# Attention and quantized feed-forward block on one core: batch 1's rotary products on GpSimd, statistics in pairs, maxima 8 slots ahead

## Chip, cores and metric

The kernel runs on one core of a Trainium2 chip. The metric is the device time of one execution in microseconds (us); lower is better. Engines are named as in the profile: PE (TensorE), DVE (VectorE), ACT (ScalarE), POOL (GpSimd) and SP (SyncE, which issues the DMAs).

## What is computed

The input is `x` of 8 batches x 512 rows x 256 columns. The rows are normalised (layer norm without weights); the result feeds causal attention with 16 heads of width 16 and rotary positions, and a linear layer whose input and weight are rounded to fp8 with one scale per tensor. Both are added to `x`:

```python
xn = _layernorm(x, axis=-1)
x = x + _L0_attn_ref(xn, L0_attn_W_q, L0_attn_W_k, L0_attn_W_v, L0_attn_W_o) + _L0_ffn_ref(xn, L0_ffn_weight, L0_ffn_bias)
```

and inside the two:

```python
Qr = _rope(Qh, cos, sin)
Kr = _rope(Kh, cos, sin)
scores = jnp.einsum('bhqd,bhkd->bhqk', Qr, Kr) * DH ** (-0.5)
...
pattern = jax.nn.softmax(scores, axis=-1)
heads = jnp.einsum('bhqk,bhkd->bhqd', pattern, Vh)
...
xq = fake_quant_fp8(x)
wq = fake_quant_fp8(weight)
return jnp.einsum('bsd,od->bso', xq, wq) + bias
```

The scale of the fp8 rounding needs the largest absolute value over all eight batches.

## The kernel before

All engines have their own instruction list, written out in Python, and wait on each other by semaphores; an engine never passes an instruction that waits. After a prologue the lists run over **slots**. A batch n has 20 slots, 20n to 20n+19, five for each of its four groups of heads. In a slot PE computes scores of batch n transposed (`scores`, line 864, into the two banks `st_ps`), ACT takes the exponents of them (`exp`, line 724), POOL masks the diagonal (`mask`, line 465), and PE multiplies with the values three and six slots after a group's first slot (`first_block`, `other_blocks`, line 958).

The softmax needs the row maxima first. PE computes the scores once more the other way round, two banks per slot (`scores_for_max`, line 884, into the three banks `s_ps`), and DVE takes the maxima (`row_max`, line 607). This runs `LEAD` = 10 slots ahead of the exponents, so the slot loop begins at slot -10. When a group's maxima are complete, PE turns them (`turn_max`, line 936, item `"mt"`), DVE splits them in two bf16 parts (`split_max`, lines 640 and 642), and SP writes them as two extra rows under the queries (`shift_rows`, line 358); the first scores of that group wait for these DMAs.

The queries and keys of a batch come from a chain: PE projects (item `"qk"`, `project`, line 849), DVE multiplies with cosine and sine (`rope`, lines 555 and 556), then `rotate` (lines 307, 308), `high` (705), `remainder` (315), `middle` (710) and `low` (320) split the result in three bf16 parts, with w = 0 for queries and w = 1 for keys. From batch 1 on, POOL does rotate, remainder and low, and ACT high and middle. SP writes the parts to DRAM (`write_parts`, line 333) and reads them back in the layout of the scores (`read_stack`, line 349). Batch 0 has its own short chain ahead of the slot loop (`project_whole`, line 839).

Where the smaller pieces stand is a table, `OFFSETS` (line 48): an item and the slot, relative to 20n, at which PE does it. Items (`"qk"`, `"v"` values, `"o"` heads turned back, `"at"`, `"fin"` output, `"mt"`, `"spread"`) take two shared banks `m_ps` in turn, and `bank_free` (line 974) makes PE wait until the item two places earlier has been read by its reader: ACT for `"v"` (`copy_v`, line 731) and `"at"`, DVE for the others. `copy_v` stands in ACT's list one slot after its item. `copy_heads` (738) of the last group stands two slots into the next batch.

The prologue also has the row statistics of all eight batches (`statistics`, lines 533 to 541, DVE; `invert`, 434 and 436, POOL; `normalise`, 692, ACT; `turn_rows`, 829, PE; `copy_turned`, 699, ACT), spread over slots -10 to -3 for batches 3 to 7 (`TURN_SLOT`). The rounding of the normalised input runs over steps qv (ACT), qe, qc (DVE), qw, xq (POOL) at slots set by `quant_at` (line 105). In an engine's list a slot's pieces stand in a fixed order; on ACT it is: exponents of the slot, turned copies, qv, `copy_heads` of the last group, `copy_v` of the item one slot earlier, `copy_at`, the other `copy_heads`, and last high and middle of the chain.

## Time and profile before

| what | value |
|---|---|
| median of 3 runs | 444.62 us (443.45 to 444.95) |
| the profiled execution: its own time | 446.0 us |
| the profiled execution: span from first to last instruction | 444.0 us |
| busy share PE, DVE, ACT, POOL | 89%, 81%, 63%, 64% |
| mean granted TensorE clock | 0.965 |
| share of the chain that ended last: PE, DVE, ACT, DMA | 59%, 17%, 8%, 5% |

Busy shares are averages over stages that differ. The span has three: the prologue up to the first row maxima, a stretch in which maxima run without exponents and the first two batches settle, and then batches that repeat to a hundredth of a microsecond.

### The profile page before, as it was taken

To read this page: it belongs to the slowest core of one execution; us is meant where nothing else is said; L and a number is where in the kernel's file an instruction comes from. 1 tells how busy PE (TensorE), PEld (TensorE's weight loads), DVE (VectorE), ACT (ScalarE), POOL (GpSimd) and SP (SyncE) were. 2 spreads that over 40 slices of the span, in tenths; PEclk is the share of its full clock that TensorE was granted. 3 is DMA by queue.
4 is the path that set the end of the run, shared out by engine and by line. 5 is a ranking of instruction groups with operands and counts; after the bars stand their busy time and mean duration, and the time that the engine had idled before them with its cause. 6 is when DMAs were issued, how large, how long until landed. Compare 5 with 4: busy or idle time off the path is not lost.

```text
span 444.0 us, 9396 instructions
## 1 busy us (share of the span) xinstructions
PE 397.3 (89%) x2911; PEld 234.7 (53%) x2911; DVE 359.3 (81%) x1372; ACT 278.9 (63%) x505; POOL 282.8 (64%) x284
## 2 busy tenths in 40 slices
PE   7905778987989999999999999999999999999886
PEld 7504553443645655565656565565555554555435
DVE  1997789999797879988898889888988898779314
ACT  3564758564773777567765766677747766657651
POOL 2575685367576678668767786687866764236670
PEclk9956899997998999999999999999999999999999
DMA  8939425833186047733675257623970497020111
GB/s 265 290 130 230 68 74 135 162 62 120 53 162 145 2 131 203 141 54 120 178 140 90 73 172 157 128 74 118 192 144 21 149 211 144 9 95 2 34 64 47
DMA packets 34049, 53.16 MB, mean 120 GB/s; under 512 B 4496, under 2 KB 30480, under 8 KB 31120
## 3 DMA queue, kind: packets, MB, share of 16 engines
q1 hardware_dynamic: 34000, 52.57, 48.3%
q8 instruction: 23, 0.38, 0.4%
q14 instruction: 26, 0.21, 0.2%
HBM read 35.52 MB, written 16.78 MB: 118 GB/s over the span
## 4 chain that ended last, share of the span: by engine, by line
PE 59%; DVE 17%; ACT 8%; issue 7%; DMA 5%; POOL 3%; SPq 1%; POOLq 0%; DVEq 0%; ACTq 0%
PE o_ps L958 13%; PE st_ps L864 12%; PE s_ps L884 9%; PE m_ps L849 8%; DVE scratch L607 8%; PE m_ps L916 5%; PE m_ps L893 5%; ACT prob L724 4%; DMA xnT<-x_dram 2%; DMA q_st<-shift 1%; PE m_ps L924 1%; DMA qk_parts<-parts 1%; POOL parts L320 1%; DVE stats L533 1%; DVE rowmax L607 1%
## 5 line engine op out<-in xcount | busy, mean ns | idle before, releaser
L607 DVE CUSTOM_DVE_ANT_0 scratch<-s_ps,causal 128x512 bf16<-128x512 f32 (+3 forms) x512 | 220.4, 484 | 36.6 <-PE s_ps L884 36.2
L724 ACT ACTIVATE prob<-st_ps 128x512 f32<-128x512 f32 x320 | 174.6, 600 | 105.4 <-PE st_ps L864 104.1
L465 POOL TENSOR_SCALAR_AFFINE_SELECT prob<-prob 128x512 f32<-128x512 f32 (+1 forms) x160 | 90.4, 569 | 122.5 <-ACT prob L724 121.8
L884 PE MATMUL s_ps<-k_st,q_st 96*128 96x512 bf16 (+3 forms) x512 | 122.9, 303 | 22.9 <-DMA k_st<-qk_parts 14.4
L864 PE MATMUL st_ps<-q_st,k_st 98*128 98x128 bf16 (+3 forms) x512 | 123.2, 304 | 10.2 <-ACT prob L724 6.2
L864 PEld LDWEIGHTS st_ps<-q_st,k_st 98*128 98x128 bf16 x512 | 41.4, 97 | 89.7 <-ACT prob L724 48.0
L958 PE MATMUL o_ps<-prob,v_sb 128*17 128x512 f32 (+3 forms) x1024 | 82.7, 440 | 1.2 <-POOL prob L465 0.7
L884 PEld LDWEIGHTS s_ps<-k_st,q_st 96*128 96x128 bf16 x512 | 49.0, 98 | 48.5 <-DVE rowmax L607 15.9
L607 DVE DVE_READ_ACCUMULATOR2_ANT rowmax<- 128x1 f32 x512 | 41.3, 81 | 0.0
L958 PEld LDWEIGHTS o_ps<-prob,v_sb 128*17 128x17 f32 x1024 | 23.0, 97 | 30.4 <-issue 26.4
L320 POOL TENSOR_TENSOR parts<-rot,parts 128x1024 bf16<-128x1024 f32 (+1 forms) x16 | 32.6, 2042 | 2.6 <-ACT parts L710 2.6
L315 POOL TENSOR_TENSOR rot<-rot,parts 128x1024 f32<-128x1024 f32 (+1 forms) x16 | 32.1, 2010 | 3.0 <-ACT parts L705 3.0
L893 PE MATMUL m_ps<-wv_sb,xnT 128*128 128x256 f32 x128 | 30.7, 382 | 0.0
L555 DVE TENSOR_TENSOR prod<-m_ps,cos_sb 128x512 f32<-128x512 f32 x30 | 22.2, 798 | 10.1 <-PE m_ps L849 9.5
L916 PE MATMUL m_ps<-wo_sb,attnT 128*128 128x256 f32 x112 | 28.8, 378 | 0.0
L849 PE MATMUL m_ps<-x_parts,wq_parts 128*128 128x512 f32 x84 | 24.6, 432 | 1.8 <-DVE shift L642 1.8
L893 PEld LDWEIGHTS m_ps<-wv_sb,xnT 128*128 128x128 f32 x128 | 23.6, 191 | 4.4 <-ACT v_sb L731 1.8
L849 PE MATMUL m_ps<-x_parts,wk_parts 128*128 128x512 f32 x84 | 24.2, 425 | 0.0
L692 ACT ACTIVATE xnT<-xnT,shift_x,rstd 128x256 f32<-128x256 f32 x32 | 16.6, 594 | 11.4 <-POOL shift_x L436 11.3
L628 DVE SCALAR_TENSOR_TENSOR x_res<-m_ps,both,x_res 128x256 f32<-128x256 f32 x28 | 13.5, 480 | 12.3 <-PE m_ps L924 12.3
L916 PEld LDWEIGHTS m_ps<-wo_sb,attnT 128*128 128x128 f32 x112 | 20.2, 189 | 2.2
L556 DVE TENSOR_TENSOR prod<-m_ps,sin_sb 128x512 f32<-128x512 f32 x30 | 21.3, 749 | 0.0
(121 smaller groups left out, 524.9 us busy)
## 6 DMA issues: line engine op xcount, KB each, us to landing
qk_parts<-parts SPq DMA_DIRECT2D x16, 768.0 KB, 4.2
q_st<-qk_parts SPq DMA_DIRECT2D x15, 384.0 KB, 6.2
k_st<-qk_parts SPq DMA_DIRECT2D x15, 384.0 KB, 6.8
xnT<-x_dram SPq DMA_DIRECT2D x8, 512.0 KB, 8.8
q_st<-qk_parts SPq DMA_DIRECT2D x15, 256.0 KB, 4.9
k_st<-qk_parts SPq DMA_DIRECT2D x15, 256.0 KB, 7.7
x_res<-x_dram SPq DMA_DIRECT2D x7, 512.0 KB, 3.3
out_dram<-x_res SPq DMA_DIRECT2D x7, 512.0 KB, 2.9
```

The lines of the kernel that those rows point to most:

```text
L315: eng.tensor_tensor(buf, buf, parts[:, w, 0, a:z, :], ALU.subtract).then_inc(rem_done[w], z - a)
L320: eng.tensor_tensor(parts[:, w, 2, a:z, :], rotated_in(n, w)[:, a:z, :], parts[:, w, 1, a:z, :], ALU.subtract).then_inc(low_done[w], z - a)
L465: eng.affine_select(out=ap, in_=ap, compare_op=ALU.is_ge, fill=0.0, base=0, pattern=pat, channel_multiplier=-1).then_inc(masked, 1)
L555: eng.tensor_tensor(a, bank[:, :], cos_sb[:, :], ALU.mult)
L607: eng.tensor_tensor_reduce(scratch[:, at % 3, col:col + w], s_ps[at % 3][:, col:col + w], causal[:, T - w:T], 1.0, NEG, ALU.add, ALU.max, ...
L724: eng.activation(prob[u][:, half * T:(half + 1) * T], st_ps[ST_BANK[2 * s + half]][:, :], ACT.Exp, scale=SCALE).then_inc(exp_done, 1)
L849: mm = eng.matmul(bank[:, :], w_parts[k // 2][:, wp, c, k % 2, :], x_parts[:, xp, c, :], start=(i == 0), stop=(i == len(terms) - 1))
L864: mm = eng.matmul(st_ps[ST_BANK[i]][:, col:col + T - kb * P], k_st[0:ROWS + SHIFT, n % 2, h, kb * P:(kb + 1) * P], q_st[0:ROWS + SHIFT, n ...
L884: mm = eng.matmul(bank[:, col:col + (qb + 1) * P], q_st[0:ROWS, n % 2, h, qb * P:(qb + 1) * P], k_st[0:ROWS, n % 2, h, 0:(qb + 1) * P], st ...
L893: mm = eng.matmul(bank[:, t * D:(t + 1) * D], xnT[:, n, c, (2 * i + t) * P:(2 * i + t + 1) * P], wv_sb[:, c, :], start=(c == 0), stop=(c = ...
L916: mm = eng.matmul(bank[:, 0:D], attnT_of(n, qb)[:, c, :], wo_sb[:, c, :], start=(first and c == 0), stop=(not first and c == NC - 1))
L958: mm = eng.matmul(o_ps[32 * i:32 * i + VW, kb * P:T], v_sb[:, kb, g * HG + i, :], prob[u][:, col:col + T - kb * P], start=(kb == 0), stop= ...
```

## The change

The change rewrites the prologue and moves items. In words:

- `LEAD` is 8, so the slot loop begins at slot -8.
- Batch 1's four projections stand in slots -6 to -3 (`EARLY`). Their bank is copied by ACT (`copy_projection`) to `x_res` and `attn`, and POOL does the products with cosine and sine from there (`rope_of_copy`). Batch 1's chain has its own slots (`EARLY_CHAIN`); the others keep theirs, but for the read of the first half of the queries, which moves from slot 2 to slot 0 of the batch ahead.
- Batch 0's `remainder` and `low` of the queries move from POOL to DVE, and its parts are written to DRAM one by one (`write_first`).
- `statistics` takes two batches at a time for 3, 4 and 5, 6; `normalise` runs two batches ahead of `copy_turned`; batch 0's `largest` stands in front of its ropes; the constants that POOL fills stand earlier.
- Item v 1 of each batch is at slot 1 and mt 1 at slot 2 (before: 2 and 1); mt 0 is one slot later; the shift rows of groups 0 and 1 are written at slots -2 and 3 (before -3 and 2), so the keys' `write_parts` of slot 2 comes in front of group 1's rows.
- The first batch's rounding steps and the weight's steps are one or two slots later, with the second `spread` at slot 19.
- PE has more idle multiplications (`keep_busy`) while it waits for batch 0's parts.

```diff
-LEAD = 10
+LEAD = 8
...
-OFFSETS = {("v", 0): 0, ("mt", 1): 1, ("v", 1): 2, ("o", 0): 23, ("o", 1): 24, ("o", 2): 25, ("o", 3): 26, ("mt", 2): 7,
+OFFSETS = {("v", 0): 0, ("v", 1): 1, ("mt", 1): 2, ("o", 0): 23, ("o", 1): 24, ("o", 2): 25, ("o", 3): 26, ("mt", 2): 7,
            ("at", 0): 28, ("qk", 0): -32, ("at", 1): 29, ("qk", 1): -30, ("fin", 0): 31, ("at", 2): 32, ("mt", 3): 12,
-           ("qk", 2): -27, ("fin", 1): 34, ("at", 3): 34, ("qk", 3): -25, ("fin", 2): 36, ("mt", 0): -4, ("fin", 3): 38}
-SPREAD = [(17, "spread", 0, 0), (18, "spread", 0, 1)]
-TURN_SLOT = {3: -10, 4: -9, 5: -7, 6: -5, 7: -3}
+           ("qk", 2): -27, ("fin", 1): 34, ("at", 3): 34, ("qk", 3): -25, ("fin", 2): 36, ("mt", 0): -3, ("fin", 3): 38}
+SPREAD = [(17, "spread", 0, 0), (19, "spread", 0, 1)]
+EARLY = {("qk", 0): -6, ("qk", 1): -5, ("qk", 2): -4, ("qk", 3): -3}
+CHAIN = {("rotate", 0): -29, ("high", 0): -28, ("remainder", 0): -27, ("middle", 0): -26, ("low", 0): -25,
+         ("write", 0): -24, ("rotate", 1): -24, ("high", 1): -23, ("remainder", 1): -22, ("middle", 1): -20,
+         ("low", 1): -19, ("write", 1): -18, ("read", 0, 0): -20, ("read", 0, 1): -16, ("read", 1, 0): -12,
+         ("read", 1, 1): -11}
+EARLY_CHAIN = {("rotate", 0): -4, ("high", 0): -3, ("remainder", 0): -2, ("middle", 0): -1, ("low", 0): 0,
+               ("write", 0): 1, ("rotate", 1): 0, ("high", 1): 2, ("remainder", 1): 3,
+               ("middle", 1): 4, ("low", 1): 5, ("write", 1): 6, ("read", 0, 0): 3,
+               ("read", 0, 1): 8, ("read", 1, 0): 9, ("read", 1, 1): 10}
+TURN_SLOT = {3: -LEAD, 4: -LEAD + 1, 5: -LEAD + 2, 6: -LEAD + 4, 7: -LEAD + 6}
...
-    first, last, loop = (23, 24, 25, 26, 28), (6, 7, 11, 12, 14), (16, 17, 21, 22, 24)
+    first, last, loop = (24, 25, 27, 28, 30), (6, 7, 11, 12, 14), (16, 17, 21, 22, 24)
...
+            def write_first(w):
+                for t, (done, out_) in enumerate(((hi_done, early_out), (mid_done, early_out), (low_done, parts_out))):
+                    eng.wait_ge(done[w], 2)
+                    eng.dma_start(qk_dram[0, w].rearrange("t r j h n -> (j h) t r n")[:, t],
+                                  parts[:, w, t]).then_inc(out_[w], 16)
...
-                for g, off in enumerate((-3, 2, 8, 13)):
+                for g, off in enumerate((-2, 3, 8, 13)):
...
+            def rope_of_copy(k):
+                eng.wait_ge(rope_copied, k + 1)
+                eng.wait_ge(cos_in, 16 * 2)
+                if k % 2 == 0:
+                    eng.wait_ge(rotated[1 - k // 2], 2 + 2 * (k // 2))
+                a, c = rope_places(k)
+                eng.tensor_tensor(a, rope_in(k), cos_sb[:, :], ALU.mult)
+                eng.tensor_tensor(c, rope_in(k), sin_sb[:, :], ALU.mult).then_inc(roped, 1)
...
-            for n in range(4):
+            for n in range(3):
                 statistics(n)
-            eng.wait_ge(w_qk_in, 16 * 4)
+            largest(0)
+            eng.wait_ge(cos_in, 16 * 2)
             rope(0, 0, first_ps[0])
             rope(0, 1, first_ps[1])
             rotate(eng, 0, 0)
             rope(0, 2, first_ps[2])
+            remainder(eng, 0, 0)
             rope(0, 3, first_ps[3])
             rotate(eng, 0, 1)
+            low(eng, 0, 0)
             remainder(eng, 0, 1)
             low(eng, 0, 1)
-            for n in range(4, NB):
-                statistics(n)
+            statistics(3, 4)
+            statistics(5, 6)
...
+            def copy_projection(k, bank):
+                eng.wait_ge(full["qk"], 4 + k + 1)
+                eng.copy(rope_in(k), bank[:, :]).then_inc(rope_copied, 1)
...
                     copy_turned(n)
-                    if n + 1 < NB:
-                        normalise(n + 1)
+                    if n + 2 < NB:
+                        normalise(n + 2)
+                for k in [k for _, n, k in shared_at(slot, "qk") if n == 1]:
+                    copy_projection(k, shared["qk", 1, k])
...
-            keep_busy(26)
+            keep_busy(22)
             turn_rows(0)
-            keep_busy(8)
+            keep_busy(6)
...
             turn_rows(2)
+            keep_busy(20)
+            eng.wait_ge(low_done[1], 2)
+            keep_busy(16)
+            eng.wait_ge(parts_out[1], 16)
+            keep_busy(10)
```

The lists read as follows at three places; line numbers are those of each kernel. In these rows `prod` holds the products of the ropes, `rot` the rotated half, `parts` the bf16 parts, `prob` the exponents.

Ahead of slot 0, POOL before, from the remainder of batch 1's queries to the first masks:

```order
L315 TENSOR_TENSOR rot<-rot,parts 128x1024 [waits hi_done0,rotated0]
L320 TENSOR_TENSOR parts<-rot,parts 128x1024 [waits mid_done0]
L439 MEMSET k_st 2x4096 [waits low_done0,ln_rstd]
L307 TENSOR_TENSOR rot<-prod 128x512 [waits low_done0,roped,consts]
L308 TENSOR_TENSOR rot<-prod 128x512
L315 TENSOR_TENSOR rot<-rot,parts 128x1024 [waits hi_done1,rotated1]
L465 AFFINE_SELECT prob<-prob 128x2x128 [waits exp_done] x2
```

and POOL with the change, from the first product of batch 1's first projection to the first mask:

```order
L495 TENSOR_TENSOR prod<-x_res,cos_sb 128x512 [waits rotated1,cos_in,rope_copied]
L496 TENSOR_TENSOR prod<-x_res,sin_sb 128x512
L495 TENSOR_TENSOR prod<-x_res,cos_sb 128x512 [waits cos_in,rope_copied]
L496 TENSOR_TENSOR prod<-x_res,sin_sb 128x512
L333 TENSOR_TENSOR rot<-prod 128x512 [waits low_done0,low_done1,roped]
L334 TENSOR_TENSOR rot<-prod 128x512
L495 TENSOR_TENSOR prod<-attn,cos_sb 128x512 [waits rotated0,cos_in,rope_copied]
L496 TENSOR_TENSOR prod<-attn,sin_sb 128x512
L495 TENSOR_TENSOR prod<-attn,cos_sb 128x512 [waits cos_in,rope_copied]
L496 TENSOR_TENSOR prod<-attn,sin_sb 128x512
L341 TENSOR_TENSOR rot<-rot,parts 128x1024 [waits hi_done0,rotated0]
L516 AFFINE_SELECT prob<-prob 128x2x128 [waits exp_done]
```

The eight products of batch 1 now stand on POOL between its rotate, remainder and the first mask, and the second rotate has moved behind that mask. ACT with the change, from the last `normalise` (batch 7) to the first exponent:

```order
L759 ACTIVATE xnT<-xnT,shift_x,rstd 128x256 [waits ln_rstd]
L759 ACTIVATE xnT<-xnT,shift_x,rstd 128x256 x3
L781 COPY x_res<-m_ps 128x512 [waits qk_full] x2
L766 COPY xnT<-st_ps 128x512 [waits xn_turned]
L766 COPY xnT<-o_ps 128x512
L781 COPY attn<-m_ps 128x512 [waits qk_full] x2
L772 CAST parts<-rot 128x1024 [waits rotated0,parts_out0]
L766 COPY xnT<-st_ps 128x512 [waits xn_turned]
L766 COPY xnT<-o_ps 128x512
L777 CAST parts<-rot 128x1024 [waits rem_done0]
L795 ACTIVATE prob<-st_ps 128x512 [waits st_full,consts,w_split]
```

The copies of batch 1's projections stand behind the last `normalise`, and the first exponent behind `middle` (L777), which waits for POOL's remainder.

In batch 1's second and third slot, PE before, from the second item v to the first item o (the `heads` rows):

```order
L893 MATMUL m_ps<-wv_sb,xnT 128x256 [waits xnT_copied,v_copied]
L893 MATMUL m_ps<-wv_sb,xnT 128x256 x3
L864 MATMUL st_ps<-q_st,k_st 128x128 [waits exp_done]
L864 MATMUL st_ps<-q_st,k_st 128x384
L884 MATMUL s_ps<-k_st,q_st 128x128 [waits max_done]
L884 MATMUL s_ps<-k_st,q_st 128x384
L864 MATMUL st_ps<-q_st,k_st 128x128 [waits exp_done]
L864 MATMUL st_ps<-q_st,k_st 128x384
L884 MATMUL s_ps<-k_st,q_st 128x512 [waits max_done]
L900 MATMUL m_ps<-ident,heads 128x128 [waits heads_copied,shift_done]
```

and PE with the change, from item mt to the first item o:

```order
L1011 MATMUL m_ps<-ident,rowmax 16x128 [waits max_done,v_copied]
L939 MATMUL st_ps<-q_st,k_st 128x128 [waits exp_done]
L939 MATMUL st_ps<-q_st,k_st 128x384
L959 MATMUL s_ps<-k_st,q_st 128x512 [waits max_done]
L939 MATMUL st_ps<-q_st,k_st 128x128 [waits exp_done]
L939 MATMUL st_ps<-q_st,k_st 128x384
L959 MATMUL s_ps<-k_st,q_st 128x128 [waits max_done]
L959 MATMUL s_ps<-k_st,q_st 128x384
L975 MATMUL m_ps<-ident,heads 128x128 [waits heads_copied,v_copied]
```

Before, the item two places ahead of the first o was mt, so o waits for `shift_done` (DVE); now it is the second v, so o waits for `v_copied` (ACT). ACT at this place before, from the first to the second `copy_v`:

```order
L731 COPY v_sb<-m_ps 128x32x16 [waits pv_done,v_full]
L724 ACTIVATE prob<-st_ps 128x512 [waits st_full,pv_done]
L724 ACTIVATE prob<-st_ps 128x512 [waits st_full]
L738 COPY heads<-o_ps 128x512 [waits pv_done]
L724 ACTIVATE prob<-st_ps 128x512 [waits st_full,pv_done]
L724 ACTIVATE prob<-st_ps 128x512 [waits st_full]
L793 ACTIVATE qv<-xnT,scale 128x1024 [waits wquant]
L731 COPY v_sb<-m_ps 128x32x16 [waits v_full]
```

and with the change, over the same slots:

```order
L802 COPY v_sb<-m_ps 128x32x16 [waits pv_done,v_full]
L795 ACTIVATE prob<-st_ps 128x512 [waits st_full,pv_done]
L795 ACTIVATE prob<-st_ps 128x512 [waits st_full]
L809 COPY heads<-o_ps 128x512 [waits pv_done]
L802 COPY v_sb<-m_ps 128x32x16 [waits v_full]
L795 ACTIVATE prob<-st_ps 128x512 [waits st_full,pv_done]
L795 ACTIVATE prob<-st_ps 128x512 [waits st_full]
```

The second `copy_v` now follows the copy of the heads at once, one slot earlier than before.

In batch 1's slots 26 to 30, POOL before, over the rounding of batch 0's input (qv is step qw, xq step xq, x_res the bias):

```order
L450 TENSOR_TENSOR x_parts<-xnT,x_parts 128x1024 [waits qk_full,x_high]
L465 AFFINE_SELECT prob<-prob 128x2x128 [waits exp_done]
L510 TENSOR_TENSOR qv<-qv,qe 128x1024 [waits qc_done]
L465 AFFINE_SELECT prob<-prob 128x2x256 [waits exp_done] x2
L517 TENSOR_TENSOR xq<-qv,qe 128x1024 [waits qw_done]
L465 AFFINE_SELECT prob<-prob 128x4x128 [waits exp_done]
L522 TENSOR_TENSOR x_res<-x_res,bias_sb 128x1024 [waits res_in]
L465 AFFINE_SELECT prob<-prob 128x2x128 [waits exp_done] x2
```

and with the change:

```order
L501 TENSOR_TENSOR x_parts<-xnT,x_parts 128x1024 [waits qk_full,x_high]
L516 AFFINE_SELECT prob<-prob 128x2x128 [waits exp_done]
L516 AFFINE_SELECT prob<-prob 128x2x256 [waits exp_done] x2
L567 TENSOR_TENSOR qv<-qv,qe 128x1024 [waits qc_done]
L516 AFFINE_SELECT prob<-prob 128x4x128 [waits exp_done]
L579 TENSOR_TENSOR x_res<-x_res,bias_sb 128x1024 [waits res_in]
L516 AFFINE_SELECT prob<-prob 128x2x128 [waits exp_done]
L574 TENSOR_TENSOR xq<-qv,qe 128x1024 [waits qw_done]
L516 AFFINE_SELECT prob<-prob 128x2x128 [waits exp_done]
```

Step xq stood two masks and a bias addition earlier; it now comes behind the bias addition.

## Rows read from the trace of the kernel before

**Rows 1.** Windows: length, busy (count) of PE, PEld, DVE, ACT, POOL; PEclk; DMA; GB/s.

```profile
63.20:111.32 48.12, 40.91 (x279) 20.65 (x280) 45.70 (x165) 29.13 (x51) 27.81 (x29) 0.95 0.49 111
...
209.17:255.60 46.43, 45.62 (x349) 26.97 (x349) 40.68 (x159) 31.15 (x57) 33.83 (x33) 1.00 0.55 126
```

**Rows 2.** Timeline of PE, prologue: start, length, engine, line, operation, count, idle before.

```profile
38.50 1.03 PE L884 MATMUL s_ps<-k_st,q_st 96*128 96x512 bf16 x3 [14.45 <-DMA k_st<-qk_parts]
```

**Rows 3.** Timeline of DVE, prologue.

```profile
17.35 2.96 DVE L555 TENSOR_TENSOR prod<-m_ps,cos_sb 128x512 f32<-128x512 f32 x1
...
20.41 0.69 DVE L307 TENSOR_TENSOR rot<-prod 128x512 f32<-128x512 f32 x1
```

**Rows 4.** Chain that ended last: batch 0's keys to DRAM (start, length).

```profile
30.28 4.33 DMA qk_parts<-parts
```

**Rows 5.** Timeline of POOL, prologue.

```profile
16.76 3.51 POOL L439 MEMSET k_st<- 2x4096 f32 x1
...
46.94 1.27 POOL L308 TENSOR_TENSOR rot<-prod 128x512 f32<-128x512 f32 x1
...
49.94 2.14 POOL L315 TENSOR_TENSOR rot<-rot,parts 128x1024 f32<-128x1024 f32 x1
```

**Rows 6.** Timeline of ACT, prologue to slot 0.

```profile
36.21 2.08 ACT L692 ACTIVATE xnT<-xnT,shift_x,rstd 128x256 f32<-128x256 f32 x4 [3.73 <-POOL shift_x L436]
...
64.13 1.08 ACT L724 ACTIVATE prob<-st_ps 128x512 f32<-128x512 f32 x2
```

**Rows 7.** Timeline of PE: slots 9, 18, 21 and 40 begin; slot 28's projection.

```profile
82.94 0.39 PE L864 MATMUL st_ps<-q_st,k_st 98*128 98x256 bf16 x2
...
105.10 0.38 PE L864 MATMUL st_ps<-q_st,k_st 98*128 98x128 bf16 x2
...
114.83 0.38 PE L864 MATMUL st_ps<-q_st,k_st 98*128 98x512 bf16 x1
...
133.64 2.93 PE L849 MATMUL m_ps<-x_parts,wq_parts 128*128 128x512 f32 x6 [0.50 <-DVE shift L642]
...
162.74 0.38 PE L864 MATMUL st_ps<-q_st,k_st 98*128 98x512 bf16 x1 [0.18 <-ACT prob L724]
```

**Rows 8.** Timeline of DVE: maxima of slot 9 begin; one `largest`.

```profile
84.77 0.27 DVE L607 CUSTOM_DVE_ANT_0 scratch<-s_ps,causal 128x128 bf16<-128x128 f32 x1
...
95.30 1.20 DVE L545 TENSOR_REDUCE amax<-xnT 128x1 f32<-128x1024 f32 x1
```

**Rows 9.** Timeline of POOL, a repeating batch's slot 29: the bias.

```profile
232.94 2.37 POOL L522 TENSOR_TENSOR x_res<-x_res,bias_sb 128x1024 f32<-128x1024 f32 x1
```

**Rows 10.** Timeline of PE, the same batch: slots 2, 3, 5 and 11.

```profile
215.16 1.93 PE L893 MATMUL m_ps<-wv_sb,xnT 128*128 128x256 f32 x8
...
217.81 0.60 PE L900 MATMUL m_ps<-ident,heads 128*128 128x128 f32 x4
...
220.65 0.38 PE L864 MATMUL st_ps<-q_st,k_st 98*128 98x512 bf16 x1
...
235.82 0.38 PE L924 MATMUL m_ps<-wf_q,xq 128*128 128x256 bf16 x2
```

**Rows 11.** Timeline of ACT, the same batch, slots 1 to 3.

```profile
214.46 0.58 ACT L731 COPY v_sb<-m_ps 128x512 f32<-128x512 f32 x1 [1.13 <-PE o_ps L958]
...
215.90 0.61 ACT L738 COPY heads<-o_ps 128x512 f32<-128x512 f32 x1
...
218.38 0.59 ACT L731 COPY v_sb<-m_ps 128x512 f32<-128x512 f32 x1
```

**Rows 12.** Tile shift over two batches: its DMAs, issue to landing.

```profile
DMA to landing us min/median/max: 1.6/1.7/3.2
```

**Rows 13.** Timeline of SP: the keys' write is issued, the same batch.

```profile
216.02 0.36 SPq L333 DMA_DIRECT2D qk_parts<-parts  x1
```

**Rows 14.** DMA issues, 209 to 232 us: count, KB each, median us to landing.

```profile
qk_parts<-parts SPq DMA_DIRECT2D x1, 768.0 KB, 4.6
...
q_st<-qk_parts SPq DMA_DIRECT2D x2, 384.0 KB, 5.8
```

More of the change, by code:

```diff
@@ L92, in batch_at, with chain_at @@
     return n if rest == 0 and first <= n < NB else None
+def chain_at(slot, *step):
+    if slot == EARLY_CHAIN[step]:
+        return 1
+    return batch_at(slot, CHAIN[step], 2)
 def residual_at(slot, loop, last):
@@ L226, in attention_ffn_block @@
         w_qk_in = sem("w_qk_in")
+        cos_in = sem("cos_in")
         w_in = sem("w_in")
@@ L403, in _ @@
                         shift_rows(n, g)
-                for off, step in ((-24, lambda n: write_parts(n, 0)), (-18, lambda n: write_parts(n, 1)),
-                                  (-18, lambda n: read_stack(n, 0, 0)), (-16, lambda n: read_stack(n, 1, 0)),
-                                  (-12, lambda n: read_stack(n, 0, 1)), (-11, lambda n: read_stack(n, 1, 1))):
-                    n = batch_at(slot, off, 1)
+                for w in range(2):
+                    n = chain_at(slot, "write", w)
                     if n is not None:
-                        step(n)
+                        write_parts(n, w)
+                for i, w in ((0, 0), (0, 1), (1, 0), (1, 1)):
+                    n = chain_at(slot, "read", i, w)
+                    if n is not None:
+                        read_stack(n, w, i)
                 n = batch_at(slot, 39)
@@ L805, in _ @@
                         copy_heads(n, g)
-                for off, step, w in ((-28, high, 0), (-26, middle, 0), (-23, high, 1), (-20, middle, 1)):
-                    n = batch_at(slot, off, 1)
+                for name, step, w in (("high", high, 0), ("middle", middle, 0), ("high", high, 1), ("middle", middle, 1)):
+                    n = chain_at(slot, name, w)
                     if n is not None:
```

136 lines of the change are left out of this document (82 added, 54 removed).

## The prediction

> **What bounds the kernel now.** I read the windows first, because they tell where a saved microsecond can still be seen at the end. In a repeating batch PE is busy 45.62 of 46.43 us [rows 1]: here PE is the bound, seven such batches fill most of the span, and whatever makes PE wait once in a batch is paid seven times. Between slot 0 and slot 20 it is another engine: DVE is busy 45.70 of 48.12 us while PE has 40.91 [rows 1]. So the reader should keep three stages apart. Ahead of slot 0 a chain over several engines sets the time, in slots 9 to 18 it is DVE, and after about slot 40 it is PE.
>
> The prologue was read next, along the chain. PE stands idle for 14.45 us until the keys of batch 0 have come back from DRAM, and then starts the first row maxima at 38.50 [rows 2]. The first exponents follow at 64.13 [rows 6]. In between DVE makes ten slots of maxima and all ropes of batch 1. Last, I followed one repeating batch on PE and ACT side by side [rows 10, 11], since two items change places there.
>
> **The sum, term by term.** All times of the trace belong to the profiled execution, whose own time is 446.0 us, 1.4 above the median of 444.62. The sum is made against 446.0 and the 1.4 is taken off at its end.
>
> *1. The way to the first maxima.* DVE's products start at 17.35 [rows 3], behind four batches of statistics. With the change three batches and one `largest` (1.20, [rows 8]) stand ahead, and I put the start at 15.9. Twenty half-tile operations follow on DVE, since the queries' remainder and low have come over from POOL. One takes 0.69 [rows 3]; they overlap a little, so 0.6 to 0.69 each gives an end between 27.9 and 29.7, and I take 28.6. Before, the keys' write began at 30.28 and took 4.33 for all three parts [rows 4]. Now only the last third is left to write then. It costs between a third of that (1.4) and all of it; I take 2.4, so it lands at 31.0. From there to the first maxima it was 3.9 (38.50 less 34.61, [rows 2, 4]), so they begin at 34.9, **3.6 earlier**. This isn't carried into the sum, because the next term is set elsewhere.
>
> *2. The way to the first exponents.* They now stand in ACT's list behind `middle` of batch 1's queries, and that waits for POOL. Before, ACT reached the next `normalise` at 36.21, 5.9 after the keys' low, with POOL's inverse as the last to come [rows 6]. In the change a pair of statistics makes it longer and a `split_x` less ahead of the inverse makes it shorter; I take 5.4, so 34.0. Five `normalise` at 2.0 and three turned copies at 1.0 each (two halves like ACT's `copy_v` of 0.58, [rows 11]) bring ACT to 47.0, and the first copy of a projection to 47.6. POOL then does eight products and two halves of a rotate, ten operations at 1.23 (1.27 long, [rows 5]), and a remainder at 2.14 [rows 5]: 14.4, so 62.0. `middle` takes one more. First exponents at 63.1, **1.0 earlier**. The bounds are 61.0, if copies and products overlap with the last `normalise`, and 65.0, if statistics of batch 7 hold the last one.
>
> *3. Slots 0 to 9.* The rotate of the keys (2.5), their remainder and both lows (2.1 each) now stand among the first masks, and no longer in front of them. Slot 9 began at 82.94 [rows 7], 18.8 after the first exponents. What POOL has gained is 6.7 if all of it shows, and nothing if all of it is covered. Laying POOL's list end to end with the masks gives 21.5, **+2.7**, so slot 9 at 84.6.
>
> *4. Slots 9 to 18.* They took 22.16 [rows 7], and DVE set the pace. Its maxima of slot 9 began at 84.77 [rows 8], 1.8 behind PE's start of the slot: DVE was late by then. With slots 0 to 9 slower and DVE's products gone from the front it has caught up, and I let it begin 0.5 behind PE, 1.3 better. One `largest` less stands in the stretch, 1.1 from its start to the next one's [rows 8]. Together **−2.4**, so that slot 18 stands at −0.7. This is the term I trust least: its ends are 0, if DVE is as late as before and others set the pace, and −3.6, the whole of term 1.
>
> *5. Slots 18 to 21.* These took 9.73 [rows 7] against 7.0 for three mean slots of a repeating batch [rows 1]. The weight's scale steps and the second `spread` are the cause, and they move apart by one slot. Ends 0 and −2.7; I take **−2.0**.
>
> *6. Batch 1.* From slot 21 to slot 40 it took 47.91 [rows 7]; nineteen mean slots of a repeating batch are 44.1 [rows 1], so 3.8 can be won at most. Of that a wait of 0.50 for the split maxima and a projection that took 2.93 [rows 7] are one place: PE waits for a split that stands behind the rounding step qc on DVE. qc is a slot later now; I take −3.0. On the other side xq stands behind the bias addition on POOL, which takes 2.37 [rows 9], and the first output matmul waits for xq: +2.3. Net **−0.7**, ends −3.8 and +2.3.
>
> *7. The repeating batches.* Item v 1 (1.77 from start to start, 1.93 long, [rows 10]) now stands in slot 1, ahead of `other_blocks`; the maxima's item of 0.2 leaves that place. ACT's first `copy_v` waits for `other_blocks` and started at 214.46 [rows 11]; that becomes 216.0. From its start to the end of the copy of the heads it was 2.05 [rows 11], and the second `copy_v` now follows there at 0.59 [rows 11]: its end is at 218.6. The first item o on PE, which before waited for DVE and started at 217.81 [rows 10], now needs exactly this copy, because the item two places ahead of it is the second v. **+0.8 in each batch**, less 0.2 for a small wait that the later mt 0 fills: 0.6 by seven batches, **+4.2**. Ends: 0, if ACT gets the copy done in time after all, and +5.6.
>
> *8. The tail* has two slots with maxima that had none: **+0.4** (two slots had ended in about 2 each, a mean slot has 2.3, [rows 1]).
>
> From −1.0 (term 2) by +2.7, −2.4, −2.0, −0.7, +4.2 and +0.4 the sum is **+1.2**: 447.2 against 446.0, and 445.8 against the median.
>
> Costed at nothing: the reads of the queries, moved two slots ahead, because their first use is eight slots later; the keep-busy multiplications, because PE waits there anyway.
>
> **The rivals.**
>
> *R1, the start keeps its gain: faster.* If POOL doesn't hold the first exponents, the chain ends with DVE: first maxima 3.6 earlier and two slots of maxima fewer ahead of slot 0, at 1.3 each, make slot 0 about 6.2 earlier in place of 1.0. DVE then takes back part of it in slots 9 to 18, to where slot 18 stands 6.2 earlier, 5.5 better than forecast: **440.3**. For it: DVE was the busiest there [rows 1]. Against it: eight products on POOL at 1.23 are 9.8 in one line [rows 5], and the exponents stand behind them in ACT's list.
>
> *R2, the shift rows come late: slower.* SP writes the keys' 768 KB in front of group 1's rows. In the same batch the write was issued at 216.02 [rows 13] and landed 4.6 later [rows 14], at 220.6. With the change the rows are issued at about 218.5 and needed when slot 5 starts, at 220.65 [rows 10] plus 0.8. Rows alone land in 1.7, which is in time; the slowest took 3.2 [rows 12], 0.3 late; and the reads that now stand in front of the write took 5.8 [rows 14], which would put the write at 221.5 to 222.8 and the rows behind it. I price it at 0.8 in six batches: +4.8, **450.6**. It decides when the rows land more than 2.9 after the split. The Trainium skill (DMA: Bandwidth & Descriptors, § Queues, rings and completion order) says that on each engine descriptors are consumed in ring order, which would put the rows behind the write; by that this rival would be the likelier, and no row here shows the two in this order.
>
> *R3, no new wait: faster.* Term 7 is nothing, as ACT's copies run ahead: 445.8 − 4.2 = **441.6**. For it: ACT is busy only 31.15 of 46.43 [rows 1]. Against it: ACT's copy was itself waiting for PE, 1.13 [rows 11].
>
> *R4, DVE held by a memset: slower.* POOL's memset of 3.51 [rows 5] now stands behind the first inverse, at 14.6 to 18.1, over DVE's statistics of batch 2. In the trace the product at 17.35 lasted 2.96, to the end of the memset at 20.27 [rows 3, 5], but the rotate behind all four products starts at 20.41 [rows 3]: they had run under the memset, and only their ends came late. So I book no delay. If they were held from their start instead, DVE's chain would begin at 18.9 in place of 15.9 and terms 1 and 2 shift by 3.0: **448.8**. The Trainium skill (SBUF — State Buffer, § Who interferes with whom) states such a lock: VectorE in a two-port mode and GpSimd take the shared ports for a whole instruction, and the second fully blocks. By that rule it would come out at this rival; the four products under one memset speak against it.
>
> **How the numbers follow.** The forecast has 0.38, R1 0.17, R2 0.22, R3 0.15, R4 0.08. A measurement of this kernel tells about 0.3% from no change, 1.3 us: faster is below 443.3, slower above 446.0. R1, R3 and the forecast's lower tail (0.04) make faster 0.36. Half of the rest of the forecast (0.17) and the mild end of R2 (0.03) make same 0.20. The remainder is slower, 0.44. The range goes from 440.0, just below R1, to 451.0, just above R2. The forecast's own range is 443 to 448.5, from terms 3 to 6.
>
> **What would show it.** Right: first maxima near 34.9; POOL's first product near 47.6; first exponents at 63; slot 18 at 104.4 and slot 21 near 112; in every repeating batch a PE wait in front of the first item o, released by ACT's `copy_v`, and a period of 47.0 in place of 46.43; DMA as releaser of slot 5 nowhere. Wrong: first exponents before 60 (R1), a wait for a DMA of the shift rows at slot 5 (R2), a period of 46.4 or less (R3), or first products of batch 0 later than 18 on DVE (R4).

## The result, and the profile after

The changed kernel is slower: 456.27 us in the median of four runs (452.93 to 459.28) beside 444.19 (443.45 to 444.95) for the kernel before, a ratio of 1.027 (95% interval 1.0195 to 1.0345). The forecast was 445.8, with a range to 451.0. Its own runs lie 6 us apart, so single medians of versions of it tell a difference of 1 or 2 us badly; what follows is read from stages of the profiles, and from intervals where these part.

The prologue came out nearly as forecast. The timelines of the changed kernel (start, length, engine, line, operation; in brackets the idle time before and what ended it), one engine each, begin with PE. They answer to [rows 2]:

```profile
34.80 0.61 PE L959 MATMUL s_ps<-k_st,q_st 96*128 96x512 bf16 x3 [0.35 <-DMA k_st<-qk_parts]
...
56.76 0.61 PE L939 MATMUL st_ps<-q_st,k_st 98*128 98x512 bf16 x1 [4.50 <-ACT xnT L766]
...
63.47 0.39 PE L939 MATMUL st_ps<-q_st,k_st 98*128 98x512 bf16 x1 [1.74 <-ACT prob L795]
...
75.88 0.61 PE L939 MATMUL st_ps<-q_st,k_st 98*128 98x512 bf16 x1 [3.20 <-DMA q_st<-shift]
...
86.47 0.39 PE L939 MATMUL st_ps<-q_st,k_st 98*128 98x256 bf16 x2
```

Then DVE [rows 3] (its first product, and the first maxima of slot 9, as in [rows 8]), POOL [rows 5] and ACT [rows 6]:

```profile
15.63 0.68 DVE L615 TENSOR_TENSOR prod<-m_ps,cos_sb 128x512 f32<-128x512 f32 x1
...
88.19 0.40 DVE L667 CUSTOM_DVE_ANT_0 scratch<-s_ps,causal 128x256 bf16<-128x256 f32 x1
```

```profile
46.95 1.31 POOL L495 TENSOR_TENSOR prod<-x_res,cos_sb 128x512 f32<-128x512 f32 x1 [2.66 <-ACT x_res L781]
...
59.64 2.14 POOL L341 TENSOR_TENSOR rot<-rot,parts 128x1024 f32<-128x1024 f32 x1
```

```profile
61.87 1.04 ACT L777 CAST parts<-rot 128x1024 bf16<-128x1024 f32 x1 [5.17 <-POOL rot L341]
62.82 2.16 ACT L795 ACTIVATE prob<-st_ps 128x512 f32<-128x512 f32 x4
...
74.69 1.04 ACT L777 CAST parts<-rot 128x1024 bf16<-128x1024 f32 x1 [1.90 <-POOL rot L341]
```

DVE's products start at 15.63, the first maxima at 34.80, POOL's first product at 46.95, the first exponents at 62.82: 1.3 earlier than before, behind the remainder on POOL and `middle`. From there on it goes wrong. These are the windows of both kernels by the same slots: 0 to 9, 9 to 18, 18 to 21, 21 to 40 and 40 to 159 (columns as in [rows 1]). First the kernel before:

```profile
63.20:82.94 19.74, 17.73 (x120) 9.25 (x120) 17.89 (x69) 13.71 (x24) 11.26 (x12) 1.00 0.57 121
82.94:105.10 22.16, 17.96 (x138) 9.11 (x135) 22.06 (x75) 12.61 (x22) 13.07 (x14) 1.00 0.46 102
105.10:114.83 9.73, 8.73 (x40) 4.63 (x38) 8.93 (x36) 6.28 (x11) 4.12 (x5) 0.65 0.23 70
114.83:162.74 47.91, 45.13 (x337) 25.86 (x335) 39.21 (x149) 30.64 (x55) 34.22 (x33) 0.96 0.44 101
162.74:430.07 267.33, 259.05 (x2003) 149.91 (x2004) 220.72 (x873) 177.99 (x326) 180.16 (x178) 1.00 0.48 113
```

and the changed one:

```profile
56.76:86.47 29.71, 24.32 (x121) 12.27 (x122) 17.50 (x66) 15.00 (x25) 20.76 (x19) 0.75 0.26 81
86.47:108.33 21.86, 18.99 (x139) 9.95 (x135) 20.91 (x70) 11.82 (x21) 12.41 (x14) 0.92 0.64 138
108.33:115.35 7.02, 6.10 (x39) 3.36 (x38) 6.80 (x30) 6.13 (x10) 5.11 (x6) 1.00 0.41 138
115.35:167.77 52.42, 46.91 (x337) 25.65 (x335) 39.65 (x156) 31.81 (x57) 32.86 (x32) 0.93 0.38 87
167.77:441.01 273.24, 262.15 (x2010) 149.29 (x2011) 224.53 (x886) 177.58 (x326) 177.97 (x178) 1.00 0.45 111
```

Slot 0 begins 6.4 earlier and slot 9 is 3.5 later; slot 21 is level again (+0.5). Then batch 1 loses 4.5 and the repeating batches with the tail's slots 5.9. That is +10.9 of the 11.0 between the spans (455.0 and 444.0).

What PE waited for, in total, times and the longest, from slot 0 on, in the changed kernel:

```profile
PE st_ps L939 <- DMA q_st<-shift: 8.9, 9, 3.2
PE st_ps L939 <- ACT prob L795: 8.4, 21, 2.1
PE st_ps L939 <- ACT xnT L766: 4.5, 1, 4.5
PE m_ps L975 <- ACT v_sb L802: 2.5, 7, 0.4
PE m_ps L999 <- POOL xq L574: 2.1, 1, 2.1
```

The shift rows had held the kernel before for 2.8 in all; the waits for `copy_v` and xq are new. PE's timeline has two pairs in batch 1 that the reader should see together, a wait and what runs behind it:

```profile
129.25 0.39 PE L939 MATMUL st_ps<-q_st,k_st 98*128 98x512 bf16 x1 [2.08 <-ACT prob L795]
...
131.69 2.08 PE L1033 MATMUL o_ps<-prob,v_sb 128*17 128x384 f32 x24
...
146.50 0.56 PE L999 MATMUL m_ps<-wf_q,xq 128*128 128x256 bf16 x2 [2.06 <-POOL xq L574]
146.99 2.76 PE L1033 MATMUL o_ps<-prob,v_sb 128*17 128x384 f32 x24
```

The same `other_blocks` take 1.49 in a repeating batch (at 221.44): the work behind each wait runs slower, and the mean granted clock of slots 21 to 40 is 0.93.

### The profile page after: what moved, and what is told of

It is laid out like the page before. It is cut to its first block, busy times and chain, and to the rows that moved or that the text cites. A ratio compares the mean times of both kernels' runs of the same rounds, so it can differ in the third digit from the quotient of the medians.

```text
span 455.0 us, 9577 instructions
## 1 busy us (share of the span) xinstructions
PE 411.8 (91%) x2991; PEld 242.3 (53%) x2991; DVE 357.1 (78%) x1368; ACT 280.9 (62%) x509; POOL 284.6 (63%) x288
## 4 chain that ended last, share of the span: by engine, by line
PE 56%; DVE 16%; issue 9%; DMA 6%; ACT 6%; POOL 5%; SPq 1%; DVEq 0%; ACTq 0%; POOLq 0%
PE o_ps L1033 13%; PE st_ps L939 11%; PE s_ps L959 8%; PE m_ps L924 7%; DVE scratch L667 7%; PE m_ps L968 6%; PE m_ps L991 5%; DMA q_st<-shift 4%; ACT prob L795 4%; PE m_ps L999 1%; DMA xnT<-x_dram 1%; POOL prod L496 1%; DVE rowmax L667 1%; ACT v_sb L802 1%; PE m_ps L975 1%
## 5 line engine op out<-in xcount | busy, mean ns | idle before, releaser
L516 POOL TENSOR_SCALAR_AFFINE_SELECT prob<-prob 128x512 f32<-128x512 f32 (+1 forms) x160 | 86.8, 547 | 134.9 <-ACT prob L795 134.3
L939 PE MATMUL st_ps<-q_st,k_st 98*128 98x128 bf16 (+3 forms) x512 | 125.3, 307 | 22.5 <-DMA q_st<-shift 8.9
L1033 PE MATMUL o_ps<-prob,v_sb 128*17 128x512 f32 (+3 forms) x1024 | 84.5, 449 | 1.2 <-POOL prob L516 0.7
L968 PE MATMUL m_ps<-wv_sb,xnT 128*128 128x256 f32 x128 | 33.1, 405 | 0.0
L346 POOL TENSOR_TENSOR parts<-rot,parts 128x1024 bf16<-128x1024 f32 x14 | 30.4, 2170 | 0.0
L341 POOL TENSOR_TENSOR rot<-rot,parts 128x1024 f32<-128x1024 f32 x14 | 29.8, 2132 | 0.0
L968 PEld LDWEIGHTS m_ps<-wv_sb,xnT 128*128 128x128 f32 x128 | 25.6, 205 | 4.8 <-issue 0.3
L896 PE MATMUL s_ps<-ident 128*128 128x128 f32 x148 | 19.4, 295 | 4.0 <-POOL causal L467 2.5
L777 ACT CAST parts<-rot 128x1024 bf16<-128x1024 f32 (+1 forms) x16 | 15.8, 994 | 9.9 <-POOL rot L341 9.8
L896 PEld LDWEIGHTS s_ps<-ident 128*128 128x128 f32 x148 | 18.8, 210 | 4.2 <-POOL causal L467 2.5
```

The costliest lines, as they stand in the source:

```text
L341: eng.tensor_tensor(buf, buf, parts[:, w, 0, a:z, :], ALU.subtract).then_inc(rem_done[w], z - a)
L346: eng.tensor_tensor(parts[:, w, 2, a:z, :], rotated_in(n, w)[:, a:z, :], parts[:, w, 1, a:z, :], ALU.subtract).then_inc(low_done[w], z - a)
L516: eng.affine_select(out=ap, in_=ap, compare_op=ALU.is_ge, fill=0.0, base=0, pattern=pat, channel_multiplier=-1).then_inc(masked, 1)
L896: eng.matmul(s_ps[2][:, 0:P], ident[:, :], ident[:, :], start=True, stop=True)
L939: mm = eng.matmul(st_ps[ST_BANK[i]][:, col:col + T - kb * P], k_st[0:ROWS + SHIFT, n % 2, h, kb * P:(kb + 1) * P], q_st[0:ROWS + SHIFT, n ...
L968: mm = eng.matmul(bank[:, t * D:(t + 1) * D], xnT[:, n, c, (2 * i + t) * P:(2 * i + t + 1) * P], wv_sb[:, c, :], start=(c == 0), stop=(c = ...
```

## The experiments

All are edits of the changed kernel, unless said otherwise. Theory 1 held that the loss is several separate waits; theory 2 that it is the shorter lead.

**Group 1's rows in batch 0.** `("read", 0, 0)` of `EARLY_CHAIN`:

```diff
-("read", 0, 0): 3,
+("read", 0, 0): 5,
```

> Edit: the read of batch 1's queries (first half) stands at slot 5 in place of 3, so it no longer follows group 1's shift rows of batch 0 at once. Theory 1 (separate waits): the 3.2 us wait of PE for these rows at slot 5 is 1.9 the reads' doing, so it falls to about 1.3; slot 9 starts near 84.6 in place of 86.5 and the whole is 1.5 to 2 us faster. Theory 2 (the maxima are too late because only 8 slots of them run ahead): the wait at slot 5 becomes shorter too, but DVE sets slots 9 to 18, slot 18 stays near 108.3 and the end moves by less than 0.5 us.

Measured 455.82 us (ratio to the kernel before 1.0265, 1.0206 to 1.0324), and the rows still waited for, 3.0. The edit did not do what it was for: SP doesn't wait for slots, and its timeline has the reads behind the rows as before.

```profile
71.57 1.14 SPq L394 DMA_DIRECT2D q_st<-shift  x2
72.75 2.49 SPq L385 DMA_DIRECT2D q_st<-qk_parts  x3
```

So the edit tells nothing about the reads; what other traces tell of them stands in the last section.

**The keys' write.**

```diff
-("write", 1): -18,
+("write", 1): -17,
```

> Edit: from batch 2 on the keys' parts are written at slot 3, behind group 1's shift rows, as in the kernel before. Theory 1: the waits for the shift rows at slots 45, 65, 85 and so on (1.4 us in the first, 0.2 in most) go, batch 2 is 1.5 us shorter and the whole 2 to 3 us faster; slots 0 to 40 are unchanged. Theory 2: the rows are late because the maxima are, the waits stay, and the end moves by less than 0.5 us.

455.46 us (1.025, 1.0194 to 1.0305). The wait of 1.4 at slot 45 went, slots 40 to 60 took 47.27 in place of 48.37; but the next batch still took 47.28. What the write in front of the rows costs isn't shown by this: in the other versions that kept it there the wait at slot 45 ranged from none (the xq edit that follows) to 2.11 (mt 1 in front of v 1). It is not what made the period long.

**xq.**

```diff
-    first, last, loop = (24, 25, 27, 28, 30), ...
+    first, last, loop = (24, 25, 27, 28, 29), ...
```

> Edit: batch 0's step xq stands at slot 29 in front of the bias addition, not at slot 30 behind it. Theory 1: PE's wait of 2.06 us for xq ahead of the first output goes, and with it the half clock of the 1.3 us of work behind it; slot 40 starts about 3.3 us earlier (near 164.5) and the end is 3 us faster. Theory 2 or any theory in which batch 1 is late through its maxima: PE waits for DVE or ACT at slots 31 to 33 in place of POOL, and under 1 us is won.

453.91 us (1.0219, 1.0133 to 1.0305; runs from 450.5 to 456.7). In the profile the wait is gone and slots 31 to 32 take 3.5 in place of 7.2, so the price of that wait with the clock behind it was 3.7. PE still waits for ACT at slot 26.

This trace also tells something that the edit was not made for. It changes nothing ahead of slot 29, yet in this execution the rows of slot 5 came in time, and PE waited for ACT one slot later:

```profile
72.35 0.39 PE L939 MATMUL st_ps<-q_st,k_st 98*128 98x512 bf16 x1 [0.33 <-DMA q_st<-shift]
...
76.88 0.61 PE L939 MATMUL st_ps<-q_st,k_st 98*128 98x512 bf16 x1 [3.48 <-ACT prob L795]
```

Slot 9 began at 86.46 all the same (86.47 in the changed kernel). So the wait of 3.20 for rows at slot 5 isn't what made slots 0 to 9 long: without it PE stands as long for the exponents of slot 5.

**mt 1 in front of v 1.**

```diff
-("v", 0): 0, ("v", 1): 1, ("mt", 1): 2,
+("v", 0): 0, ("mt", 1): 2, ("v", 1): 2,
```

> Edit: item mt 1 stands in slot 2 in front of v 1, and v 1 goes back to slot 2, so that the first item o waits for DVE's split and not for ACT's copy. Theory 1: PE's waits for copy_v (0.36 us seven times) and for the exponents of slot 3 (0.17) go and the repeating batches take about 46.6 us in place of 47.28: 4 to 5 us faster in all. Rival: v 1 is not what costs; the period stays above 47.1 because the shift rows of group 1 are late, and the end moves by less than 1.5 us.

454.92 us (1.0236, 1.0174 to 1.0299). The period fell to 47.02 in late batches, not to 46.6. The wait for `copy_v` gave way to another one at the same instruction:

```profile
321.27 0.66 PE L975 MATMUL m_ps<-ident,heads 128*128 128x128 f32 x4 [0.49 <-DVE shift L704]
```

With mt 1 in slot 2, DVE's split stands behind the step qc and slot 2's maxima, so either order makes PE wait. Theory 1 had the wait right, but this remedy puts another in its place.

**The lead.** `LEAD` 10 with the old slots of mt 0, mt 1, v 1 and the rows:

```diff
-LEAD = 8
+LEAD = 10
...
-("v", 1): 1, ("mt", 1): 2,
+("mt", 1): 1, ("v", 1): 2,
```

> Edit: the changed kernel with 10 slots of maxima ahead again, mt 1 and v 1, mt 0 and the shift rows of groups 0 and 1 at their old slots; batch 1's ropes stay on POOL. Theory 1 (POOL's products and the chain behind them set the first exponents and slots 0 to 9): first exponents still near 62.8 us, slots 0 to 9 still take 27 to 30 us from slot 0 to 9, and only the repeating batches get back to about 46.5: the end 4 to 6 us faster than the changed kernel, near 451. Theory 2 (the lead of 8 is what costs): the waits for shift rows at slots 5, 15 and 45 go, slots 9 to 18 get shorter, and the whole comes to 446 or less.

454.13 us (1.0218, 1.0192 to 1.0243). Neither total came (451, and 446 or less); of each theory one half holds. Slots 40 to 159 take 266.40 in place of 273.24, and the period is 46.4 again: all of that loss belongs to the lead with the items that moved along with it. But the start gets worse, slot 18 at 113.28 in place of 108.33, since PE waits longer for the first exponents, and then for batch 1's keys, whose reads are timed for a lead of 8:

```profile
64.19 0.61 PE L939 MATMUL st_ps<-q_st,k_st 98*128 98x512 bf16 x1 [6.56 <-ACT prob L795]
...
93.70 0.61 PE L959 MATMUL s_ps<-k_st,q_st 96*128 96x512 bf16 x1 [4.44 <-DMA k_st<-qk_parts]
```

**ACT's list in slots 4 and 5.**

```diff
-("middle", 1): 4, ("low", 1): 5, ("write", 1): 6,
+("middle", 1): 5, ("low", 1): 6, ("write", 1): 7,
```

> Edit: batch 1's middle of the keys on ACT at slot 5 in place of 4, low and the keys' write one slot later too. It no longer stands in front of slot 5's exponents and no longer makes them wait for POOL's remainder. Theory 1: PE's wait for ACT or for the rows before slot 6 shrinks, its clock isn't halved behind it, slot 9 starts 2 to 3 us earlier (near 84) and the end is about 2 us faster. Rival: the shift rows of group 1 hold slot 5 anyway, slot 9 stays above 86 and the end moves by less than 0.5 us.

453.82 us (1.0211, 1.0179 to 1.0243). Slot 9 began at 81.62, 4.9 earlier, more than expected: in the changed kernel `middle` stood ahead of slot 5's exponents and waited 1.90 for POOL's remainder. The rows of slot 5 came in time here too (0.30 of waiting), so the fair comparison is with the xq edit above, where they did as well: 4.8. But slot 18 was only 0.8 earlier (107.53), because slot 15 waited for its rows:

```profile
100.19 0.61 PE L939 MATMUL st_ps<-q_st,k_st 98*128 98x512 bf16 x1 [4.28 <-DMA q_st<-shift]
```

These rows were issued 3.2 earlier than in the changed kernel (94.32 for 97.53), but took 4.2 and 5.3 to land in place of 2.7 and 2.8; DVE was busy for 21.65 of the 25.91 there. So the gain was given back to transfers, not to DVE; why they were slow stays open.

**The products on DVE**, from the banks, as in the kernel before:

```diff
-                for k in [k for _, n, k in shared_at(slot, "qk") if n == 1]:
-                    rope_of_copy(k)
...
-                for kind, n, k in [i for i in shared_at(slot, "qk", "o", "fin", "mt") if i[:2] != ("qk", 1)]:
+                for kind, n, k in shared_at(slot, "qk", "o", "fin", "mt"):
```

> Edit: batch 1's products with cosine and sine are done by DVE from the banks, without ACT's copies and POOL's eight products; all the rest of the changed kernel stays, the lead of 8 too. Theory 1: POOL is rid of 10.2 us in its list ahead of the first mask, DVE had idled there (4.2 and 4.7 us), so the first exponents come 6 to 8 us earlier (55 to 57), slot 9 near 79, slot 18 at 104 or earlier, and the whole is 4 to 7 us faster, near 450. Theory 2 (lead): DVE gets the products and is late with the maxima; slot 18 stays at 107 to 109 and less than 1.5 us is won at the end.

453.88 us (1.0202, 1.0162 to 1.0241). First exponents at 57.61, slot 18 at 105.93, 2.4 earlier. The median is 2.4 below the changed kernel's, and the intervals overlap. Smaller than expected, as the start now waits 1.89 for group 0's rows, and slots 5 and 15 for theirs (2.9 and 2.1).

**The same with the write, xq and mt 1 edits above.**

> Edit: the last one together with the keys written behind the shift rows, xq in front of the bias addition, and mt 1 in front of v 1 in slot 2. Theory 1: the gains add up: about 5 us from the products, 4 to 5 from xq with its clock, 3 to 4 from the repeating batches, so 441 to 444, level with the kernel before or faster. Theory 2: the lead still costs about 1 us per batch through late rows, and it stays above 448.

444.63 us (1.0005, 0.9967 to 1.0043): level with the kernel before, and just above what Theory 1 expected (441 to 444).

**Those three edits with the products left on POOL.**

> Edit: the changed kernel with batch 1's products left on POOL and the other three edits (keys written behind the shift rows, xq in front of the bias, mt 1 in front of v 1). Theory 1: against the version with the products on DVE and the same three (444.6) it shows the products' price alone, 2 to 3 us: about 447. Rival: slots 9 to 18 are set by DVE and take the gain back, so the products on POOL cost less than 0.7 us at the end.

448.54 us (1.0092, 1.0059 to 1.0126). Against 444.63 the products on POOL cost 3.9 between the medians, more than either theory had, and the intervals don't touch. In the two profiled executions it is 3.3 at slot 18 and 1.3 at the end, so the size is less sure than the sign.

**Lead 10 and lead 9 with the products on DVE** and xq in front of the bias; mt, v 1 and the rows at their old slots.

> Edit: 10 slots ahead with the old slots of mt, v 1 and the shift rows, batch 1's products on DVE, xq in front of the bias; what stays of the change is the prologue (statistics in pairs, batch 0's parts written one by one, constants early). Theory 1 (three separate losses: xq with its clock, the products on POOL, and a lead of 8 in the repeating batches): all three are gone, the repeating batches take 46.4 to 46.6 us, slot 18 starts at 104 to 106, and the whole is 440 to 444. Rival: the prologue itself costs too, slot 18 starts behind 107 and the whole stays above 446.

> Edit: as the one before, with 9 slots ahead; group 1's maxima are then done in slot 0, so mt 1 can still stand in slot 1. Theory 1: what costs in the repeating batches is that mt 1 has to go behind slot 1, not the lead as such, so they take 46.4 to 46.6 us here too, and the start is shorter by one slot of maxima (1 to 2 us) than with 10: 439 to 443. Rival: the shift rows are late with 9 as well; waits for them stay at slots 5, 15 and 45 and the period is above 46.8.

447.42 (1.0065, 1.0037 to 1.0093) and 443.72 us (0.9969, 0.9937 to 1.0002). Their periods are 46.43 and 46.50: with mt 1 in slot 1 a lead of 9 does as well as 10, so it is not the lead as such, but that a lead of 8 pushes mt 1 out of slot 1. Both medians lie above what was expected (440 to 444, 439 to 443). With 10, PE waits 4.23 for batch 1's keys again, with 9 it is 1.70; and in both, slots 21 to 40 still take 49.4 (47.91 in the kernel before), which the last experiment takes up.

**xq in the kernel before**, nothing else:

```diff
-    first, last, loop = (23, 24, 25, 26, 28), ...
+    first, last, loop = (23, 24, 25, 26, 30), ...
```

> Edit: the kernel before with nothing but batch 0's xq moved from slot 28 to slot 30, behind the bias addition. Theory 1: PE waits for POOL ahead of the first output and works at half clock behind it, as in the changed kernel: 3 to 5 us slower than the kernel before, all of it between slots 28 and 33. Rival: the loss at that place in the changed kernel comes from its later rounding steps as a whole (24, 25, 27, 28), and xq alone costs the kernel before under 1.5 us.

447.49 us (1.006, 1.003 to 1.0089): 2.8 slower, and the wait is the one of the changed kernel to a hundredth:

```profile
143.51 0.39 PE L924 MATMUL m_ps<-wf_q,xq 128*128 128x256 bf16 x2 [2.06 <-POOL xq L517]
143.83 1.49 PE L958 MATMUL o_ps<-prob,v_sb 128*17 128x384 f32 x24
```

The half clock that the theory expected behind it did not come: `other_blocks` take 1.49 here, not 2.76, the granted clock is 1.00 from 143.5 to 148, and slots 21 to 40 are 2.2 longer, the wait and hardly more.

**All rounding steps back** in the changed kernel: the second spread, the weight's steps on DVE, ACT and POOL, and `first` as before.

> Edit: the changed kernel with the weight's steps, the second spread and batch 0's rounding steps all back at the slots of the kernel before; the lead of 8, the products on POOL and the order of v 1 and mt 1 stay. Theory 1 (the later steps only moved batch 1's stall: from the half-clocked projection at slot 28 to the exponents at slot 26 and to xq at slot 31): the waits of 2.08 and 2.06 us at slots 26 and 31 go, slots 18 to 21 get back to 9.5, slots 21 to 40 to 48, and the whole is 1 to 3 us faster, 453 to 455. Rival: the later steps were a gain and only xq was wrong; slots 21 to 40 stay above 50 and the whole is not faster.

453.27 us (1.0204, 1.017 to 1.0238), 3.0 below the changed kernel, with intervals that overlap; in the profiles slot 40 begins 3.45 earlier. Slots 21 to 40 take 46.83 in place of 52.42 with the clock at 1.00, both waits are gone, and slots 18 to 21 give back 1.8. But the stall of slot 28 did not come back, as it would have to if the later steps had only moved it: with all steps at their old slots, 28 to 29 takes 4.79 (6.87 in the kernel before, 4.19 in the changed one), though PE waits for the split as before:

```profile
136.84 1.65 PE L924 MATMUL m_ps<-x_parts,wq_parts 128*128 128x512 f32 x6 [0.58 <-DVE shift L704]
```

The projection takes 1.65 here and took 2.93 there [rows 7], where the granted clock was 0.50 from 134 to 136. So most of the gain at slot 28 is the clock. Why it stayed up here is not shown.

**POOL's two operations on the weight one slot earlier**, in the version with lead 9:

```diff
-                if slot == 23:
+                if slot == 22:
```

> Edit: the version with 9 slots ahead and the products on DVE, with POOL's two operations on the weight at slot 22 in place of 23. Theory 1: ACT's step qv waits for these (1.01 us) and holds the exponents of slot 25 behind it, so PE's wait at slot 26 falls from 2.4 to about 1.3 us and the half clock behind it with it; 1 to 2 us faster, 441.5 to 443. Rival: ACT's own work (qv, the high part of the input) holds the exponents; the wait stays above 2 us and the time within 0.5 us of 443.7.

439.68 us (0.988, 0.9855 to 0.9905): the best version, faster than both kernels. ACT's qv before (lead 9) and PE behind it:

```profile
123.23 1.15 ACT L864 ACTIVATE qv<-xnT,scale 128x1024 f32<-128x1024 f32 x1 [1.01 <-POOL wf_q L561]
```

```profile
125.86 0.39 PE L935 MATMUL st_ps<-q_st,k_st 98*128 98x512 bf16 x1 [2.41 <-ACT prob L793]
...
128.17 2.24 PE L1029 MATMUL o_ps<-prob,v_sb 128*17 128x384 f32 x24
```

and with POOL's operations earlier:

```profile
120.75 1.15 ACT L864 ACTIVATE qv<-xnT,scale 128x1024 f32<-128x1024 f32 x1
```

```profile
123.39 0.39 PE L935 MATMUL st_ps<-q_st,k_st 98*128 98x512 bf16 x1 [1.29 <-ACT prob L793]
```

qv no longer waits, and the wait at slot 26 fell from 2.41 to 1.29, as expected. The gain is larger than expected, 4.0. Of the 4.0 by which slot 40 begins earlier in the profile, 2.7 lie in slots 21 to 40, where the clock stays at 1.00 behind the shorter wait (0.97 before); the other 1.4 lie ahead of slot 21, where the edit does nothing, and are not shown to be its doing.

## Why the prediction was wrong, point by point

- **Terms 1 and 2 held.** 34.80 for 34.9, 62.82 for 63.1. The rival of a held DVE (R4) fell: the first product started at 15.63. R1 fell at the same place, the exponents stood behind POOL's products.
- **Term 3, +2.7, was 4.8.** From the first exponents slot 9 took 23.65 in place of 18.8. I counted POOL's operations, and missed that ACT's `middle` waits for one of them ahead of slot 5's exponents; moving it alone won 4.8 to 4.9 there.
- **Term 4, −2.4, was −0.3.** The step that failed is "it has caught up": DVE could not work ahead, since PE, which computes the scores for the maxima in the same list, stood at the waits of slots 0, 1 and 5 (4.50, 1.74, 3.20). DVE was busy 17.50 of 29.71 there, and still began the maxima of slot 9 at 88.19, 1.7 behind PE (86.47), where I had 0.5 and the kernel before 1.8; then it was busy 20.91 of 21.86. Only the 1.1 for one `largest` less came (22.06 of 22.16 before). The group whose maxima end at slot 1 got them only after the first exponents.
- **Term 5, −2.0, was −2.7**; in the kernel before that stretch had a clock of 0.65.
- **Term 6, −0.7, was +4.5, the largest miss.** The gain at slot 28 came: 28 to 29 took 4.19 in place of 6.87. That was luck in part: qc moved by two slots, not one, and with all steps back at their old slots 2.1 of these 2.7 stayed, because the clock did. The step that failed is that I named only the split and xq as what is late next. The price of xq alone was right (2.3; in the kernel before 2.2 by the stage and 2.8 by the medians); in the changed kernel it was 3.7 with the clock. What I had left out stood on ACT: qv waits for the weight on POOL, now two slots later, the exponents of slot 25 stand behind qv, and PE waited 2.08 for them at slot 26 and lost the clock as well. The runs with the steps put back, and with POOL's two operations moved by one slot, show both.
- **Terms 7 and 8, +4.6, were +5.9.** The mechanism was right, its parts were not: of the 0.85 in one batch 0.35 are the wait for `copy_v` where I had 0.8, and 0.17 that for slot 3's exponents; the rest stands in no wait that the profile lists, the rows at slot 5 (R2's place) included. All of it goes when mt 1 is back in slot 1 (46.4 with a lead of 10, 46.5 with 9), and less than half by swapping mt 1 and v 1 (47.0).
- **R2** had the sign, but its mechanism cost little. PE waited 8.9 for rows in all, 5.4 of it up to slot 20, where the write doesn't stand in front of them; the write can explain the 1.4 at slot 45. In batches 3 to 5 the rows did land late, 2.0 to 2.6 behind their issue for 1.7 [rows 12], and about when the write in front of them landed, which agrees with the ring order quoted in R2; but none of these three waited for them at slot 5. In batch 0 the rows of group 1 were issued late because their maxima were. R3 fell.

By runs the rounding steps cost some 3 (the run with all put back), the products on POOL 3.9, and the repeating batches 5.9 to 6.8. These are not shares of the 12.1: gains stand against them (slots 18 to 21 alone are 2.7 shorter), and they don't simply add, since with a lead of 10 alone the start took the gain back. Undone together they give more: the best version lies 16.6 below the changed kernel and 4.9 below the kernel before, most of the latter in slots 18 to 21 (6.63 for 9.73).

## What to carry to other kernels

When a step is moved later, follow not only its reader but what stands behind that reader in its engine's list: here POOL's weight held qv, qv held exponents, and those held PE. A lead is only worth what the engine that fills it can work ahead: PE's own waits stopped the maxima too. And price a wait of 2 us twice, without and with slower work behind it: the same 2.06 us for xq came to 2.2 in the kernel before, where the clock stayed up, and to 3.7 in the changed one, where it fell.
